# New engine orders in the feed-forward and query rounds, and a turned up product in the expert slots, of a two-layer Perceiver kernel

## The reference, cut to what matters

```
x = x + window_attention(norm(x), ctx)        # layer 0, 16 heads of 16
x = x + causal_self_attention(norm(x))
x = x + ffn_fp8(norm(x))                      # rows scaled, rounded to 8 bits, @ W (256x256), + bias
x = x + cross_attention(norm(x), ctx, mask)   # layer 1, 257 keys
x = x + mix(norm(x))                          # gate * U * cumsum(V) and a 3-tap convolution
x = x + shared_expert(norm(x)) + sum of the 2 best of 8 experts
# ffn_fp8: s = max|x| / 448;  q = fp8(x / s);  out = (q * s) @ (W * ws).T + bias
# expert:  gelu(x @ w1[e] + b1[e]) @ w2[e] + b2[e],  w1 256x512, w2 512x256
```

## Time and profile before

| | us |
|---|---|
| median of 3 runs | 1084.53 (1083.72 to 1085.75) |
| the profiled execution | 1083.43 |
| its span | 1081.6 |
| TensorE busy | 970.9 (90%) |
| VectorE / ScalarE / GpSimd busy | 659.4 / 420.1 / 378.7 |

### The profile page before, as it was taken

How to read it: one execution, slowest core, us unless ns; L and a number is a source line. 1 busy time by engine, 2 the same in 40 slices (tenths; PEclk the granted TensorE clock), 3 DMA queues, 4 the chain that set the end, 5 groups by cost and what they waited for, 6 DMA issues and landing times.

```text
span 1081.6 us, 40633 instructions
## 1 busy us (share of the span) xinstructions
PE 970.9 (90%) x16760; PEld 745.9 (69%) x16790; DVE 659.4 (61%) x1780; ACT 420.1 (39%) x1057; POOL 378.7 (35%) x569
## 2 busy tenths in 40 slices
PE   3899899998366999999999999998798889999999
PEld 2677777776233888888888888886487556666666
DVE  3778798887841666666666666665654634444436
ACT  1223223322545555565565555563342212222211
POOL 5422223220874333334443433331314124444420
PEclk9999999999568999999999999998796999999999
DMA  7002300000001111111111211100642011111116
...
DMA packets 29745, 63.06 MB, mean 58 GB/s; under 512 B 5872, under 2 KB 22320, under 8 KB 26128
## 3 DMA queue, kind: packets, MB, share of 16 engines
...
...
## 4 chain that ended last, share of the span: by engine, by line
PE 79%; issue 8%; ACT 4%; DVE 4%; POOL 3%; DVEq 1%; SPq 0%; DMA 0%; ACTq 0%; another core or an unknown queue 0%; PEldq 0%; POOLq 0%
PE psum L820 13%; PE psum L1533 7%; PE psum L1541 6%; PE psum L893 6%; PE psum L303 5%; PE psum L882 4%; PE psum L276 4%; PE psum L338 3%; PE psum L908 3%; PE psum L329 3%; PE psum L316 3%; PE psum L1409 3%; ACT x_p L977 2%; PE psum L1190 2%; PE psum L1525 2%
## 5 line engine op out<-in xcount | busy, mean ns | idle before, releaser
L977 ACT ACTIVATE x_p<-x_s,x_nmax 128x257 f32<-128x257 f32 x256 | 127.4, 499 | 111.8 <-DVE x_nmax L1008 111.8
L1039 DVE COPY x_pT<-psum 128x512 f32<-128x512 f32 x128 | 88.2, 689 | 67.7 <-PE psum L893 65.4
L1008 DVE CUSTOM_DVE_ANT_0 x_s<-psum,x_mask 128x257 f32<-128x257 f32 x256 | 93.7, 422 | 42.2 <-PE psum L882 41.7
L893 PE MATMUL psum<-ident,x_p 128*128 128x128 f32 x512 | 80.0, 279 | 7.9 <-ACT x_p L977 1.7
L1533 PE MATMUL psum<-me_w,me_in 128*128 x156 | 77.1, 616 | 5.0 <-ACT me_in L1553 0.6
L1064 POOL TENSOR_TENSOR x_ctx1l<-x_ctx,x_ctx1h 128x2128 fp32r<-128x2128 f32 x8 | 37.9, 4732 | 113.3 <-ACT x_ctx1h L763 113.3
L1541 PEld LDWEIGHTS psum<-me_w,me_out 128*128 128x128 f32 x312 | 59.2, 190 | 25.3 <-issue 19.3
L1064 POOL TENSOR_TENSOR x_ctx0l<-x_ctx,x_ctx0h 128x2128 fp32r<-128x2128 f32 x8 | 37.8, 4726 | 107.4 <-ACT x_ctx0h L763 100.6
L1541 PE MATMUL psum<-me_w,me_out 128*128 x312 | 73.8, 379 | 0.9 <-DVE me_out L1588 0.9
L1619 POOL DMA_INDIRECT moe_outs<-me_out,me_goal x39 | 38.6, 990 | 96.0 <-DVE me_out L1580 96.0
L993 DVE TENSOR_SCALAR x_k<-psum,x_bk 128x258 f32<-128x258 f32 x128 | 57.6, 481 | 23.9 <-PE psum L820 22.9
(11 more groups left out here) (289 smaller groups left out, 2535.6 us busy)
## 6 DMA issues: line engine op xcount, KB each, us to landing
...
```

The costliest lines, as they stand in the source:

```text
L893: mm = nc.tensor.transpose(psum[:, 6, (2 * r + k) * P:(2 * r + k + 1) * P], x1_p[:, column(b, CB * c + r), k * P:(k + 1) * P], ident[:])
L977: nc.scalar.activation(x1_p[:, n, :], x1_s[:, rg, :], ACT.Exp, bias=x1_nmax[:, par, n:n + 1], scale=-1.0, accum_out=x1_sum[:, par, n:n + 1 ...
L1008: nc.vector.tensor_tensor_reduce(out=x1_s[:, rg, :], in0=psum[:, 2 + rg, 0:SK], in1=x1_mask[par][:, b, :], scale=1.0, scalar=-2 * MASKED, ...
L1039: nc.vector.tensor_copy(x1_pT[:, c].rearrange("p r k s -> p (r k s)"), psum[:, 6, :]).then_inc(x1["pT_ready"], 1)
```

## The change

Statistics: `pool_rstd` has the factors folded together; two dependent steps go. Small layers' drain: ScalarE normalises round 0 behind its last Exp, VectorE takes the scales and the rounding constants of round 0 inside its last three steps. Rounds: normalise runs two rounds ahead, behind the copies of q; the query normalise becomes `queries_normalise`, ahead of these copies; GpSimd adds rounding constants before the bias; statistics group two comes first. The first context low part moves from GpSimd to VectorE, the first spread queries move ahead of the last statistics, and the first key and value pieces ahead of the last query group, `x1_tensor` no longer waiting there for all queries. Slots: the up product holds blocks of the expert's weights (copied by VectorE to a fixed place, `me_up`, two slots ahead) and streams the turned rows, so the hidden values come out with hidden channels on partitions. ScalarE applies Gelu with the bias per partition straight from PSUM into `me_hT`; the bias addition, the four transposes and the copy go, and the hidden-bias table shrinks from [128, 8, 512] to [128, 8, 4]. The loop turns slot i+1's rows between slot i's up and slot i-1's down product. The other parts of the diff rename (`scales` to `ffn_scales`, `piece` to `x1_piece`) or move code unchanged.

```diff
-            done(nc.gpsimd.tensor_scalar(diff, diff, 0.25, None, ALU.mult))
...
-            done(nc.gpsimd.tensor_tensor(both, mean, rstd, ALU.mult))
-            nc.gpsimd.tensor_scalar(ln_shift[:, own], both, -1.0, None, ALU.mult).then_inc(ln_ready, 1)
+            nc.gpsimd.tensor_tensor(shift, both, rstd, ALU.mult).then_inc(ln_ready, 1)
...
+                if n(0)[0] == len(smalls) * NT + 1:
+                    ffn_normalise(act, 0)
...
+                if n(0)[0] == len(smalls) * NT + 2:
+                    ffn_scales(dve, 0)
+                if n(0)[0] == len(smalls) * NT + 3:
+                    ffn_magic(dve, 0)
...
         def ffn_vector(dve):
...
+                    ffn_magic(dve, i)
+                    ffn_outputs(dve, i - 1)
                 if i + 1 < ROUNDS:
-                    scales(i + 1)
+                    ffn_scales(dve, i + 1)
                 for u in range(U):
                     dve.wait_ge(f8["added"], U * i + u + 1)
                     nc.vector.tensor_tensor(f8_q[:, u, :], f8_xn[:, i % 2, u, :], f8_magic[:, u, :], ALU.subtract).then_inc(f8["q_ready"], 1)
-            outputs(ROUNDS - 1)
+            x1_context(dve, 0, 0)
+            ffn_outputs(dve, ROUNDS - 1)
...
         def ffn_pool(pool):
             pool.wait_ge(f8["w_ready"], 1)
+            pool_rstd(pool, sm["stats_ready"], NT + 3 * U, 2)
             for i in range(ROUNDS):
-                for u in range(U):
-                    t = U * i + u
-                    pool.wait_ge(f8["norm_ready"], t + 1)
-                    nc.gpsimd.tensor_tensor(x[:, t, :], x[:, t, :], f8_bias[:], ALU.add).then_inc(f8["x_biased"], 1)
-                if i == 0:
-                    pool_rstd(pool, sm["stats_ready"], NT + 3 * U, 2)
                 for u in range(U):
                     pool.wait_ge(f8["magic_ready"], U * i + u + 1)
                     v = f8_xn[:, i % 2, u, :]
                     nc.gpsimd.tensor_tensor(v, v, f8_magic[:, u, :], ALU.add).then_inc(f8["added"], 1)
                 if i == 0:
                     pool_rstd(pool, sm["stats_ready"], NT + 4 * U, 3)
+                for u in range(U):
+                    t = U * i + u
+                    pool.wait_ge(f8["norm_ready"], t + 1)
+                    nc.gpsimd.tensor_tensor(x[:, t, :], x[:, t, :], f8_bias[:], ALU.add).then_inc(f8["x_biased"], 1)
                 if i > 0:
                     pool_rstd(pool, f8["stats_ready"], U * i, i - 1)
+            x1_queries(pool, 0, 0)
             pool_rstd(pool, f8["stats_ready"], NT, ROUNDS - 1)
...
+        def ffn_normalise(act, i):
+            group_ready(act, "ffn0", i)
+            for u in range(U):
+                t = U * i + u
+                nc.scalar.activation(f8_xn[:, i % 2, u, :], x[:, t, :], ACT.Identity, bias=ln_shift[:, t:t + 1],
+                                     scale=ln_rstd[:, t:t + 1]).then_inc(f8["norm_ready"], 1)
...
-            normalise(0)
             scale(0)
+            ffn_normalise(act, 1)
             for i in range(ROUNDS):
                 if i + 1 < ROUNDS:
-                    normalise(i + 1)
                     scale(i + 1)
+                if i > 0:
+                    queries_normalise(act, i - 1)
                 for v in range(PAIRS):
                     act.wait_ge(f8["qT_done"], U * i + 2 * v + 2)
                     if i > 0:
                         act.wait_ge(f8["out_done"], U * (i - 1) + 2 * v + 2)
                     nc.scalar.activation(f8_qT[:, 2 * v:2 * v + 2, :, :].rearrange("p u k s -> p (u k s)"),
                                          psum[:, v, :].bitcast(BF16)[:, 0:2 * D], ACT.Copy).then_inc(f8["qT_ready"], 2)
-                if i > 0:
+                if i + 2 < ROUNDS:
+                    ffn_normalise(act, i + 2)
+                if i == 0:
+                    group_ready(act, "ffn0", ROUNDS - 1)
+                    for k in range(KC):
+                        context_high(act, 0, 0, k)
+                    mask(act, 0, 0)
+                else:
                     queries_scalar(act, i - 1)
-            group_ready(act, "ffn0", ROUNDS - 1)
-            for k in range(KC):
-                context_high(act, 0, 0, k)
-            mask(act, 0, 0)
+            queries_normalise(act, ROUNDS - 1)
             queries_scalar(act, ROUNDS - 1)
...
+        def x1_first_pieces(pe):
             pe.wait_ge(x1["w_split"], 4)
             for k in range(2):
                 pe.sem_inc(x1[f"kv{k}_free"], 1)
+            for n in range(LEAD, len(PIECES)):
+                x1_piece(pe, n, -1, 1, True)
...
+                if t + b + c == 0:
+                    pe.wait_ge(x1["q_ready"], KC * NT // U)
...
-                ready(pe, "s_biased", SLOTS)
+                ready(pe, "s_h_ready", SLOTS)
...
             turn(0)
             e = expert_of(pe, 0)
             for i in range(SLOTS + 1):
+                if i < SLOTS:
+                    ready(pe, "sT_ready", i + 1)
+                    ready(pe, "up_w_ready", i + 1)
+                    if i >= 2:
+                        ready(pe, "s_h_ready", i - 1)
+                    for m in range(HM):
+                        for k in range(KC):
+                            mm = nc.tensor.matmul(psum[:, i % 2, m * P:(m + 1) * P], me_up[i % 2][:, k * HID + m * P:k * HID + (m + 1) * P],
+                                                  me_sT[:, i % 2, k, :], start=(k == 0), stop=(k == KC - 1), skip_group_check=True)
+                    mm.then_inc(me["s_up_done"], 1)
+                    if i + 1 < SLOTS:
+                        turn(i + 1)
                 if i > 0:
                     ready(pe, "s_h_ready", i)
-                    if i > 2:
-                        ready(pe, "hT_ready", i - 2)
-                    for m in range(HM):
-                        mm = nc.tensor.transpose(psum[:, 2 + (i - 1) % 2, m * P:(m + 1) * P], me_sh[:, (i - 1) % 2, m * P:(m + 1) * P], ident[:])
-                    mm.then_inc(me["hT_done"], 1)
-                if i < SLOTS:
-                    ready(pe, "sT_ready", i + 1)
-                    if i >= 2:
-                        ready(pe, "s_biased", i - 1)
-                    for k in range(KC):
-                        w = me_w[:, bass.ds(e, 1), 0, k * HID:(k + 1) * HID].rearrange("p e c -> p (e c)")
-                        mm = nc.tensor.matmul(psum[:, i % 2, :], me_sT[:, i % 2, k, :], w, start=(k == 0), stop=(k == KC - 1))
-                    mm.then_inc(me["s_up_done"], 1)
-                if i > 0:
-                    ready(pe, "hT_ready", i)
                     if i > 2:
                         ready(pe, "y_ready", i - 2)
                     for m in range(HM):
...
                     mm.then_inc(me["y_done"], 1)
                 own = e
                 if i + 1 < SLOTS:
-                    turn(i + 1)
                     e = expert_of(pe, i + 1)
...
+            ready(act, "expert_ready", 1)
+            act.wait_ge(me["experts_loaded"], 16 * (E + 2))
             turn(0)
             for i in range(SLOTS):
-                ready(act, "s_biased", i + 1)
-                if i >= 2:
-                    ready(act, "hT_done", i - 1)
-                nc.scalar.activation(me_sh[:, i % 2, :], me_sb[:, i % 2, :], ACT.Gelu).then_inc(me["s_h_ready"], 1)
+                e = expert_of(act, i)
                 if i + 1 < SLOTS:
                     turn(i + 1)
+                ready(act, "s_up_done", i + 1)
+                if i >= 2:
+                    ready(act, "y_done", i - 1)
+                for m in range(HM):
+                    ins = nc.scalar.activation(me_hT[:, i % 2, m, :], psum[:, i % 2, m * P:(m + 1) * P], ACT.Gelu,
+                                               bias=me_eb1[:, bass.ds(e, 1), m:m + 1].rearrange("p e m -> p (e m)"))
+                ins.then_inc(me["s_h_ready"], 1)
...
+
+            def up_weights(i):
+                e = expert_of(dve, i)
+                if i >= 2:
+                    ready(dve, "s_up_done", i - 1)
+                nc.vector.tensor_copy(me_up[i % 2], me_w[:, bass.ds(e, 1), 0, :].rearrange("p e c -> p (e c)")).then_inc(me["up_w_ready"], 1)
+                return e
+
+            experts = [up_weights(0), up_weights(1)]
+            for i in range(SLOTS):
+                e = experts[i % 2]
+                if i + 2 < SLOTS:
+                    experts[i % 2] = up_weights(i + 2)
+                ready(dve, "y_done", i + 1)
+                if i >= SB:
+                    dve.wait_ge(y_stored[i % SB], 16 * (i // SB))
+                b = me_eb2[:, bass.ds(e, 1), :].rearrange("p e c -> p (e c)")
+                nc.vector.tensor_tensor(me_y[:, i % SB, :], psum[:, 6 + i % 2, 0:D], b, ALU.add).then_inc(me["y_ready"], 1)
...
-            me_eb1 = scratch("me_eb1", [P, E, HID])
+            me_eb1 = scratch("me_eb1", [P, E, HM])
...
+            me_up = [v[:].rearrange("p i c -> p (i c)") for v in (me_sb, me_sh)]
...
                     queries_tensor(pe, i - 1)
+            x1_first_pieces(pe)
```

214 lines of the change are left out of this document (92 added, 122 removed).

## The result

The changed kernel takes 1049.28 us, the median of four runs (1047.86 to 1052.80), against 1084.12 us (1081.22 to 1085.75, four runs) for the kernel before on the same chip. The ratio is 0.9686 (95% interval 0.9654 to 0.9718). The profiled execution took 1049.85 us with a span of 1048.1. The forecast was 1046.5, with 1039 to 1059 as the range.

What follows compares the result with a forecast made beforehand. TensorE, 79% of the chain, was taken as bounding: its own instructions in the slots, an in-order hand-over chain in the rounds. Slots -27.5, rounds -10 and first normalise -0.5 make -38, so 1046.5 us, range 1039 to 1059 (own range 1040 to 1053).

Steps and rivals of the forecast that it cites:

- The slots: Expert slots: period falls from 4.48 to 3.82 us over 39 slots, -27.5 us with the start (ends -30.6 and -20.5).
- the seam: Expert slots: a possible small cost between TensorE's products, taken as 0.08 us per slot.
- the start: Start of the expert slots: first up product waits for VectorE's register load and weight copy, +0.4 us.
- the weight copy: Expert slots: VectorE's added copy of 1024 float32 columns, 0.9 to 1.4 us, taken as 1.1, with slack.
- The test for "wrong": Wrong if first up record to last down product exceeds 156 us (149 forecast), or first Exp is later than 350.
- D: Rival, up product: weight loads not hidden behind 128 columns, 0.297 us per record, kernel slower at 1163 us; chance 0.03.
- C: Rival, slots: TensorE's register load is bared, 0.53 us per slot or 20.7 back, 1067 us; chance 0.05.
- B: Rival, slots: weight copy stalls GpSimd's indirect DMAs, period about 4.1 us, 11 back, 1057.5 us; chance 0.08.
- The rounds: Feed-forward and query rounds: shorter hand-over chain brings the first cross-attention Exp forward, -10 us (ends -5 and -13).
- the walk: Rounds: new engine orders followed with old durations; query products at 301.5, 317.3, 327.4, 337.6, first Exp at 344.0 us.
- A: Rival, rounds: ScalarE's new wait for query statistics holds TensorE each round, low clock stays; 1053.5 us, chance 0.13.
- The drain: Small layers' end: round 0 normalised behind the last Exp, so scaling comes 5.9 us and subtraction 4.5 us earlier.

Runs made afterwards that it cites:

- copies4: Changed kernel with VectorE's weight copy done four times per slot, the first three waiting for one another: 1058.24 us, ratio 0.9751.
- changed_again: The changed kernel itself run once more, nothing changed, as the scale for its scatter: 1047.40 us, ratio 0.9653.
- part2_rounds: Kernel before with everything but the slots changed (rounds' new orders and shorter statistics): 1077.02 us, ratio 0.9918.
- early_table: Changed kernel with the Exp table load moved ahead of the last query normalise: 1052.16 us, ratio 0.9696.
- table_in_wait: Changed kernel with the Exp table loaded in ScalarE's wait for the third query product: 1046.22 us, ratio 0.9632.
- pieces_back: Changed kernel with the first key and value pieces back behind the last query group: 1050.01 us, ratio 0.9667.
- copies_first: Changed kernel with ScalarE's copies of turned q and the feed-forward normalise put ahead of the query normalise: 1048.88 us, ratio 0.9646.
- stats_first: copies_first with GpSimd's query statistics also moved ahead of the same round's bias additions: 1044.34 us, ratio 0.9618.
- drain_back: Changed kernel with round 0's normalise, scales and magic numbers back behind the small layers' drain: 1056.92 us, ratio 0.9740.
- part1_slots: Kernel before with only the slots changed, rounds and statistics as before: 1055.70 us, ratio 0.9718.

## Why the prediction was right

**The slots: -27.5 forecast, -30.6 in the profiles and -30.4 alone.** The mechanism is the one forecast, and three things were sized too dearly: the seam, the start and (without effect) the weight copy. The up record was priced at 0.112 from the mix layer's convolution and took 0.111. The seam of 0.08 per slot did not appear, which is 39 x 0.09 = 3.5 us with the rounding of the record: the old up product's excess over its columns did not pass to the new one. Where it came from was not tested. The +0.4 at the start did not come either: from the end of VectorE's sums to the first up record 1.24 us passed, before 1.27. The weight copy, bounded at 0.9 to 1.4 from 256-wide operations, took 0.69. The nearest rows were four short instructions of other operations; which of the two made them dearer was not tested. (The prediction's 2.3 us of VectorE work goes with the upper bound of 1.4 for the copy; with its 1.1 the terms make 2.0.) The first two up products took 2.03 and 2.05 us, which gives 0.5 back. The test for "wrong" was 156 us; it is 146.3.

**D falls**: sixteen loads, 0.19 each, in 1.78 us. The row that the prediction set against the page's rule (the Trainium skill, TensorE: Matmul & The Clock Gate, section "The mechanism": an overlap only between different row groups) was the right guide; these are 128-row loads too and are hidden. The same section also lets a load go ahead into the background weight buffer, which the prediction did not take up; the 0.111 per record is at odds with the first rule alone. **C falls**: no gap behind the down product. The register load on TensorE's queue took 0.30 us in the median instead of the 0.53 of the earlier trace rows. It stands at 941.06 in the slot above, in the middle of the up product, as before the change, and not behind the eight down records as forecast; it was hidden either way. **B falls** by copies4.

**The rounds: -10 forecast, -9.2 in the profiles and -9.1 alone.** Counted from the last small Exp (us; the forecast's absolute marks less 264.4), since that Exp itself moved:

```
                               forecast   after   changed_again
scaling of round 0                 7.6      8.5
first query normalise may start   29.8     32.2
query product 1                   37.1     38.9    38.9
query product 2                   52.9     51.1    51.1
query product 3                   63.0     63.8    63.8
query product 4                   73.2     74.6    74.5
first Exp                         79.6     80.8    80.8
```

The order of events is the forecast's throughout: scaling behind the last turned output, the copies of q(1) held, keys ahead of the last query transposes, scores behind the last product. What failed are sizes, and one of them came right by luck: the first query product ran at full clock in this kernel, in changed_again and in part2_rounds, and at the low level in copies4 and early_table, which have the same instructions up to there, and in table_in_wait and pieces_back too. In copies4 the stretch is 83.6, and the gain of the rounds 6.5 instead of 9.2, still inside the forecast's ends of 5 and 13. The statistics came 2.4 late, in three terms. In the drain of the small layers TensorE ran at the 1.2 GHz level: the product of probabilities and values behind the last Exp took 1.90 us and the turn after it 0.69, where before they took 1.25 and 0.44. The last turned output, and the scaling behind it, stood 0.9 later than forecast for that. This is the execution's and not the change's: copies_first, pieces_back and table_in_wait have the same code there, took 1.25 and 0.44, and scaled 7.1 to 7.3 behind the last Exp. First a row of TensorE before, then the same of after:

```profile
266.21 1.25 PE L276 MATMUL psum<-sm_v,sm_pT 32*32 32x17 f32 x128 [0.81 <-DVE sm_o L403]
```

```profile
269.78 1.90 PE L274 MATMUL psum<-sm_v,sm_pT 32*32 32x17 f32 x128 [0.16 <-DVE sm_o L403]
```

The other two are GpSimd's chains of statistics: group three's took 4.9 instead of 4.3 (with its hand-over), the first query group's 5.2 instead of 4.3. Its small steps take longer beside VectorE's subtractions and rounding constants (0.31 to 0.52 instead of 0.20); GpSimd's and VectorE's timelines of after:

```profile
294.87 0.38 POOL L145 TENSOR_TENSOR ln_work<-bn_out 128x4 f32<-128x4 f32 x1
...
299.07 0.20 POOL L154 TENSOR_TENSOR ln_work<-ln_work 128x4 f32<-128x4 f32 x1
```

```profile
293.30 2.57 DVE L609 TENSOR_TENSOR f_q<-f_xn,f_magic 128x256 bf16<-128x256 f32 x4
```

The maxima put ahead of the last output's division on VectorE, which the prediction priced at 1 us with nobody waiting, held nothing: TensorE's next turn waited for another row of VectorE's (x, L410). From the statistics to the first product 6.7 us passed where the walk had 7.3, so that was 1.8 late. It ran at full clock (3.70), the second and third low (5.58, 6.07), another split than forecast; from the first to the fourth it was 35.6 us against 36.1, so that evened out.

**A falls, though its wait is real.** A had it in each round. It is 5.49 us of ScalarE, 6.22 of TensorE, in round 1 only (from round 2 on it is at most 0.52, as the argument against A had it). It cost 3.2 to 3.4 us (copies_first); with the statistics in front as well (stats_first) the stretch is 7.0 shorter. It did not eat the gain, as A had it, but sat inside the forecast, since the walk contained it.

**The drain is half of the rounds' gain, as forecast.** The forecast gave scaling and subtraction 4.5 to 5.9; drain_back against copies4, with the first product at the low level in both, puts the overlap at 4.9. The way from the last product's end to the first Exp fell by 3.3 (5.8 to 2.5), where the forecast had 3.1; the keys' place is 1.9 of it (pieces_back). The last product itself ran at full clock, 3.70 instead of 5.73, in every kernel with the new rounds, as the forecast took it: another 2.0.

**Not in the sum.** At the first Exp of the cross attention TensorE has a gap of 2.29 us, and then some 3 us at the 1.2 GHz level: +2.1 up to the first up record. The runs say where it comes from. In seven kernels the gap is 2.3 to 2.4, and in six of them the clock fell behind it (copies_first is the exception); in the six others it is 0.35 or 0.86, and the clock stayed 1.00. Behind a fall the cross attention's Exps take 396.5 to 397.2 us, without one 394.5 to 395.3. ScalarE's table load is what fills the gap: moved away, the gap is 0.86 with the keys still in front. So the early keys bring the low clock only together with the load behind them. The forecast counted the keys' gain and not this price, which is as large.

The last +0.5 is the execution's: changed_again has 31.1 there, as before. So is the +3.6 ahead of the last small Exp: over the twelve profiles of kernels with part or all of the change that mark lies anywhere from 261.4 to 268.7, part2_rounds (261.39), which has every edit to that stretch, being the lowest, and part1_slots (266.74), which has none, among the later ones. The -0.5 at the start was there (first normalise at 16.26 instead of 16.83), hidden in that scatter.

So 1046.5 against 1049.28 and 1047.40: 3.1 us too little for the slots, 0.8 too much for the rounds, 2.1 of clock that was not in the sum, and a scatter of the small layers as large as any of these. That the median came within 3 us is partly luck: the slots' 3.1 stand against 2.9 of the rounds and the clock, the rounds' own figure rests on one product at full clock, and the unchanged code behind the cross attention moves by 5 us from one execution to the next (124.2 to 129.8 over all profiles).
